# Second state-space layer: deltas from bf16 parts and a softplus read from PSUM in the scan inputs, one product block by a diagonal matrix in the scans

## Chip, core and metric

The kernel runs on one core of a Trainium2 chip. The metric is the time of one execution on the device in microseconds. The core has TensorE (PE; PEld is its weight load), VectorE (DVE), ScalarE (ACT), GpSimd (POOL) and SyncE (SP), which here only issues DMAs. Each engine takes its instructions in the order in which they are written, and the engines meet at semaphores.

## What is computed

The network has four layers on 32 images of 96 channels and 32x32 pixels. The change touches two stages of the second layer, a scan over 1024 pixels in four directions with 16 states for each of 768 channels:

```python
flat = xc.reshape(b, d, L)
flipped = xc[:, :, ::-1, ::-1].reshape(b, d, L)
xl = jnp.swapaxes(jnp.concatenate([flat, flat, flipped, flipped], axis=1), 1, 2)
A = -jnp.exp(A_log)
x_dbl = xl @ W_x                       # 6 + 16 + 16 columns
dt_r, Bm, Cm = x_dbl[..., :dr], x_dbl[..., dr:dr + n], x_dbl[..., dr + n:]
delta = jax.nn.softplus(dt_r @ W_delta + b_delta)
# for each pixel t:
dA = jnp.exp(dt[:, :, None] * A)
h = dA * h + (dt * u_t)[:, :, None] * B_t[:, None, :]
y = jnp.einsum('bdn,bn->bd', h, C_t) + Dv * u_t
```

## The kernel before

The program is a chain of stages with barriers between them; each stage loops over the 32 images.

**Scan inputs (`l1_scan_inputs`, tiles named l1p_).** The 768 channels are T = 6 tiles of 128; tiles 3 to 5 are the flipped ones and read u backwards. For an image the stage makes x_dbl on TensorE (`project`, L1258, into PSUM buffer px, in two halves of 512 pixels), copies it to SBUF on ScalarE (`read`, L1312, into dts), and makes for each tile the deltas before the softplus (`deltas`, L1265, two PSUM buffers pd). The softplus is max(x, 0) + ln(1 + exp(-|x|)): VectorE writes max(x, 0) to dl (L1228) and -|x| to ab (L1231), ScalarE does exp and ln (L1326, L1328), POOL adds the two (L1208), and VectorE multiplies by u (L1237, du). TensorE transposes du in 8 blocks (`turn_du`, L1274, into pt), ScalarE copies it out (L1320, dut), and SyncE stores dl, dut, the C rows and B. B is turned by TensorE (`turn_b`, L1280) and copied by ScalarE (L1334). The pixels of dts carry the ranks, B and C in fp32, and a product of fp32 operands is issued as two instructions for each half.

`turn(k, s)` on each engine runs through t = 0 to 5 for image k, and the function `back(k, t, lag)` says which tile stands at slot t: on TensorE the transpose of tile t-4 comes first, then the deltas of tile t+2, in slot 1 the projection of the next image, in slot 3 the turning of its B. A delta product waits until `absd` of the tile two before it, that is until VectorE has read that PSUM buffer for the last time. ScalarE's slot is: copy of tile t-5, exp and ln of t, and in slot 2 the reading of the next image's px.

**Scans (`l1_scans`, tiles named l1s_).** An image has 32 rounds (16 states, unflipped half and flipped half) of 3 tiles. For a round ScalarE makes three decays da (L1549) and eight products dm = dut x B (L1559, one for each block of 128 pixels, since B lies on the partitions there). TensorE transposes the products back, eight for each tile (L1463, into pd), VectorE scans (L1528, into h, a ring of four), POOL adds two of the three results (L1439) and multiplies twice by C (L1444, L1448), and TensorE adds these to y by products with the identity (L1473). In TensorE's order the transposes of step s+1 stand before the addition of pb (j = 1) or pa (j = 2) of the round before. After a half is done VectorE adds D times u (L1516) twice. The loop over the images is a loop of the hardware, whose body is one image.

Of the kernel before, what the change touches and what calls it, by code (L numbers as in the profile page):

```python
# [20 lines left out]
F8 = mybir.dt.float8e5  # L21
ALU = mybir.AluOpType
# [7 lines left out]
DI = 192  # L30
# [1083 lines left out]
def l1_scan_inputs(nc, u1, w, dls, duts, bts, crows, ident):  # L1114
# [4 lines left out]
    DU, TURN, OUT = 3, 4, 5  # L1119

    with ExitStack() as stack:
        r = Room(nc, "l1p", stack)
        u = r.sb("u", [128, UNROLL, 2, HW])
        dts = r.sb("dts", [128, 2, HW])
# [5 lines left out]
        wx = r.sb("wx", [128, T, 128]); wsum = r.sb("wsum", [128, 4, 128]); wd = r.sb("wd", [128, T, 128])  # L1130
# [8 lines left out]
        const, wsummed, xd, dtc, btm, btc, dtm, plus, absd, expd, lnd, sumd, dud, dutm, dutc, passed = r.step_sems(  # L1139
            "const", "wsummed", "xd", "dtc", "btm", "btc", "dtm", "plus", "absd", "expd", "lnd", "sumd", "dud", "dutm",  # L1140
            "dutc", "passed")
        consts = [(wx[:, :, :], w["wx"]), (wd[:, :, :], w["wd"]), (idt[:, :], ident)]
# [7 lines left out]
        def in_order(s, t):  # L1150
            row = u[:, s % UNROLL, U_OF[t % HT], :]
            return row[:, ::-1] if t >= HT else row

        with nc.Block() as block:
            @block.sync
            def _(sp):
# [6 lines left out]
                def turn(k, s):  # L1163
                    for t in range(T):
                        m, v = back(k, t, 3)
                        if there(m):
                            sp.wait_ge(sumd, nth(T * m + v))
                            sp.sem_inc(passed, 1)
                            sp.dma_start(one(dls[:, v], m), dl[:, v, :]).then_inc(s_dl[v], 16)
                        m, v = back(k, t, 6)  # L1170
                        if v % HT == HT - 1 and there(m):
                            g = v // HT
                            sp.wait_ge(dutc, nth(T * m + v))
# [28 lines left out]
            @block.gpsimd  # L1202
            def _(pool):
                def turn(k, s):
                    if there(k):
                        for t in range(T):
                            pool.wait_ge(lnd, nth(T * k + t))
                            pool.tensor_tensor(dl[:, t, :], dl[:, t, :], ln[:, t % 3, :], ALU.add).then_inc(sumd, 1)  # L1208

                turns(pool, turn, 1, 1)  # L1210

            @block.vector
            def _(dve):
                for rows in (slice(2 * N, 64), slice(64, 128)):
                    dve.memset(dts[rows, :, :], 1.0).then_inc(const, 1)
                dve.wait_ge(s_w, ready)
                for g in range(2):
                    dve.tensor_tensor(wsum[:, 2 * g, :], wx[:, HT * g, :], wx[:, HT * g + 1, :], ALU.add).then_inc(wsummed, 1)
                    dve.tensor_copy(wsum[:, 2 * g + 1, :], wx[:, HT * g + 2, :]).then_inc(wsummed, 1)

                def turn(k, s):
                    for t in range(T):
                        if there(k):
                            q = T * k + t
                            dve.wait_ge(s_dl[t], k * 16)
                            dve.wait_ge(dud, nth(q - T))
                            dve.wait_ge(dtm, nth(q))
                            dve.tensor_scalar(dl[:, t, :], pd[:, t % 2, :], 0.0, None, ALU.max).then_inc(plus, 1)  # L1228
                            dve.wait_ge(plus, nth(q))
                            dve.wait_ge(expd, nth(q - 3))  # L1230
                            dve.scalar_tensor_tensor(out=ab[:, t % 3, :], in0=dl[:, t, :], scalar=-2.0,  # L1231
                                                     in1=pd[:, t % 2, :], op0=ALU.mult, op1=ALU.add).then_inc(absd, 1)
                        m, v = back(k, t, DU)
                        if there(m):
                            dve.wait_ge(sumd, nth(T * m + v))
                            dve.wait_ge(dutm, nth(T * m + v - 2))
                            dve.tensor_tensor(du[:, v % 2, :], dl[:, v, :], in_order(s + (t - DU) // T, v), ALU.mult)\  # L1237
                               .then_inc(dud, 1)
# [4 lines left out]
            def _(pe):  # L1243
                pe.wait_ge(s_w, ready)
                pe.wait_ge(const, nth(1))
                pe.wait_ge(wsummed, nth(3))

                def turn(k, s):
                    p = (s + 1) % 2

                    def project():
                        pe.wait_ge(s_in[(s + 1) % UNROLL], (k + 1 - (s + 1) % UNROLL) * (16 // UNROLL) + 16)
                        pe.wait_ge(btc, nth(k))
                        for hs in HALVES:
                            for c in range(4):
                                row = u[:, (s + 1) % UNROLL, c % 2, :]
                                row = row[:, ::-1] if c >= 2 else row
                                mm = pe.matmul(px[:, hs], wsum[:, c, :], row[:, hs], start=(c == 0), stop=(c == 3))  # L1258
                        mm.then_inc(xd, 1)

                    def deltas(m, v):
                        pe.wait_ge(dtc, nth(m))
                        pe.wait_ge(absd, nth(T * m + v - 2))
                        for hs in HALVES:
                            mm = pe.matmul(pd[:, v % 2, hs], wd[:, v, :], dts[:, (s + (t + 2) // T) % 2, hs],  # L1265
# [3 lines left out]
                    def turn_du(m, v):  # L1269
                        q = T * m + v  # L1270
                        pe.wait_ge(dud, nth(q))
                        pe.wait_ge(dutc, nth(q - 1))
# [4 lines left out]
                    def turn_b():  # L1277
                        pe.wait_ge(dtc, nth(k + 1))
                        for b in range(BLOCKS):
                            mm = pe.matmul(px[:, b * N:(b + 1) * N], dts[:, p, b * 128:(b + 1) * 128], idt[:, 0:N],  # L1280
# [25 lines left out]

# [1343 lines left out]
```

## Time and profile before

| what | us |
|---|---|
| three runs | 21068.52, 21084.69 (median), 21090.51 |
| the profiled execution | 21082.77 |
| its span in the trace | 21081.0 |
| scan inputs, 9706 to 10570 | 864.0, 27.0 an image |
| scans, 10616 to 17990 | 7374.0, 230.4 an image |
| DVE, ACT, POOL, PE busy over the span | 17145.7, 16400.6, 13569.9, 18307.1 |

The two stages that the change touches are 39% of the span. The page's list of groups has the scan stage on top: 3072 scans on VectorE (6862.9 us busy), 8192 products (4459.9 us) and 3072 decays (3514.2 us) on ScalarE. Busy times of pipelined instructions overlap at their ends, so sums of durations come out above the time. Where rows carry a release ("<-PE"), it is the one that came last by the semaphores; at a loop's jump back this can name a release that had long been there.

### The profile page before, as it was taken

How to read it: one execution, taken by the hardware profiler on the slowest of the kernel's cores; microseconds unless marked ns; L12 is line 12 of the kernel's file. 1: busy time of each engine (PE TensorE's matmuls, PEld its weight loads, DVE VectorE, ACT ScalarE, POOL GpSimd, SP SyncE). 2: the span in 40 equal slices, each digit the busy share in tenths (PEclk: the TensorE clock that was granted, in tenths of full speed). 3: DMA queues.
4: the chain of work that ended last, by engine and by line, in shares of the span. 5: the costliest groups of instructions: out<-in, count | busy, mean ns of one | idle time of the engine just before them, and what ended most of it. 6: DMA issues, size and time to landing. Idle time of an engine off the chain costs nothing. (4 is left out here: it accounts for less than half of the span.)

```text
span 21081.0 us, 264592 instructions
## 1 busy us (share of the span) xinstructions
PE 18307.1 (87%) x73736; PEld 10023.1 (48%) x73736; DVE 17145.7 (81%) x12555; ACT 16400.6 (78%) x25994; POOL 13569.9 (64%) x6372
## 2 busy tenths in 40 slices
PE   7789997799985999889988998998989899789798
PEld 2345553455542344334555555555555555345353
DVE  2888888788875679748989999999999999756666
ACT  6499996799972555566799999999999999334545
POOL 0278884488861678626589999999999999100101
PEclk8799998899998999999999999999999999889899
DMA  3577775677766332276733333333333333820302
GB/s 120 189 229 219 228 229 185 208 229 220 223 206 191 106 124 78 101 251 228 272 138 123 115 124 114 125 118 121 123 115 124 114 124 117 190 68 27 89 28 83
DMA packets 842523, 3171.86 MB, mean 150 GB/s; under 512 B 101542, under 2 KB 124682, under 8 KB 816140
## 3 DMA queue, kind: packets, MB, share of 16 engines
q1 hardware_dynamic: 805900, 3030.56, 44.4%
q10 hardware_dynamic: 35328, 125.85, 1.8%
q8 instruction: 591, 9.68, 0.2%
q14 instruction: 704, 5.77, 0.1%
HBM read 2317.15 MB, written 838.88 MB: 150 GB/s over the span
## 5 line engine op out<-in xcount | busy, mean ns | idle before, releaser
L1528 DVE TENSOR_TENSOR_SCAN l1s_h<-l1s_da,l1s_pd 128x1024 f32<-128x1024 f32 x3072 | 6862.9, 2275 | 388.7 <-PE l1s_pd L1463 348.0
L1559 ACT ACTIVATE l1s_dm<-l1s_dut,l1s_bt 128x384 f32<-128x384 f32 x8192 | 4459.9, 609 | 15.9 <-DMA l1s_u<-u 11.5
L1463 PE MATMUL l1s_pd<-l1s_id,l1s_dm 128*128 128x128 f32 x24576 | 3196.2, 277 | 606.5 <-ACT l1s_dm L1559 358.6
L1463 PEld LDWEIGHTS l1s_pd<-l1s_id,l1s_dm 128*128 128x128 f32 x24576 | 2756.3, 142 | 2028.8 <-DVE l1s_h L1528 1122.7
L1549 ACT ACTIVATE l1s_da<-l1s_dl,l1s_a 128x1024 f32<-128x1024 f32 x3072 | 3514.2, 1144 | 19.1 <-DVE l1s_h L1528 18.6
L1439 POOL TENSOR_TENSOR l1s_sm<-l1s_h 128x1024 f32<-128x1024 f32 x1024 | 2429.0, 2372 | 263.8 <-DVE l1s_h L1528 253.5
L1444 POOL TENSOR_TENSOR l1s_pb<-l1s_h,l1s_cc 128x1024 f32<-128x1024 f32 x1024 | 2433.6, 2377 | 1.1
L1448 POOL TENSOR_TENSOR l1s_pa<-l1s_sm,l1s_cc 128x1024 f32<-128x1024 f32 x1024 | 2429.3, 2372 | 0.0
L852 POOL TENSOR_TENSOR dw_acc<-dw_acc,dw_prod 128x961 f32<-128x961 f32 (+3 forms) x704 | 1572.9, 2276 | 1008.2 <-ACT dw_prod L805 1000.6
L1473 PE MATMUL l1s_py<-l1s_pb,l1s_id 128*128 128x512 f32 x4096 | 1995.8, 610 | 166.3 <-POOL l1s_pb L1444 162.3
L2328 POOL TENSOR_TENSOR l0sb_pr<-l0sb_h,l0sb_cc 128x1024 f32<-128x1024 f32 x768 | 1815.8, 2365 | 434.1 <-DVE l0sb_h L2404 373.0
L2328 POOL TENSOR_TENSOR l0sf_pr<-l0sf_h,l0sf_cc 128x1024 f32<-128x1024 f32 x768 | 1815.8, 2365 | 433.7 <-DVE l0sf_h L2404 373.6
L2089 POOL CAST ffn_h<-ffn_z 128x1024 fp8e5<-128x1024 f16 x128 | 180.9, 1414 | 2897.7 <-DVE ffn_z L2109 2892.7
L1473 PE MATMUL l1s_py<-l1s_pa,l1s_id 128*128 128x512 f32 x4096 | 1927.5, 593 | 0.0
L783 PE MATMUL dw_pc<-dw_vol,dw_diag 128*128 128x512 f32 (+7 forms) x4224 | 1765.1, 581 | 57.4 <-DMA dw_vol<-n 30.4
L882 DVE SCALAR_TENSOR_TENSOR dw_pc<-dw_vol,dw_wt,dw_pc 128x961 f32<-128x961 f32 (+5 forms) x1280 | 1484.6, 1234 | 210.1 <-PE dw_pc L783 206.2
L2360 PE MATMUL l0sf_py<-l0sf_pr,l0sf_id 128*128 128x512 f32 x3072 | 1580.4, 597 | 0.0
L2360 PE MATMUL l0sb_py<-l0sb_pr,l0sb_id 128*128 128x512 f32 x3072 | 1580.3, 597 | 0.0
L2452 ACT ACTIVATE l0sf_dm<-l0sf_dut,l0sf_bt 128x192 f32<-128x192 f32 x4096 | 1500.0, 455 | 9.5 <-DMA l0sf_dl<-l0dlsf 9.5
L2452 ACT ACTIVATE l0sb_dm<-l0sb_dut,l0sb_bt 128x192 f32<-128x192 f32 x4096 | 1493.9, 447 | 9.6 <-DMA l0sb_dl<-l0dlsb 9.6
L2341 PEld LDWEIGHTS l0sb_pd<-l0sb_id,l0sb_dm 128*128 128x128 f32 x6144 | 751.7, 142 | 1105.2 <-issue 757.4
L2341 PEld LDWEIGHTS l0sf_pd<-l0sf_id,l0sf_dm 128*128 128x128 f32 x6144 | 751.5, 142 | 1105.0 <-issue 758.1
(297 smaller groups left out, 30544.0 us busy)
## 6 DMA issues: line engine op xcount, KB each, us to landing
l1s_cc<-crows SPq DMA_DIRECT2D x1024, 512.0 KB, 3.7
l0sf_cc<-l0crowsf SPq DMA_DIRECT2D x512, 512.0 KB, 5.1
l0sb_cc<-l0crowsb SPq DMA_DIRECT2D x512, 512.0 KB, 5.1
l0sf_cc<-l0crowsf SPq DMA_DIRECT2D x512, 256.0 KB, 6.6
l0sb_cc<-l0crowsb SPq DMA_DIRECT2D x512, 256.0 KB, 6.5
dls<-l1p_dl SPq DMA_DIRECT2D x192, 512.0 KB, 6.9
duts<-l1p_dut SPq DMA_DIRECT2D x64, 1536.0 KB, 5.8
l1s_dut<-duts SPq DMA_DIRECT2D x64, 1536.0 KB, 7.2
```

The lines of the kernel that those rows point to most:

```text
L783: mm = pe.matmul(pixels(pc[:, f % 4, :])[:, ys, xs], diag[:, v % tiles, diag_taps.index(tap), :], source(v, f, tap, ys, xs), start=(n == 0 ...
L1439: pool.tensor_tensor(sm[:, rnd % 2, :], h[:, rnd * HT % 4, :], h[:, (rnd * HT + 1) % 4, :], ALU.add)\
L1444: pool.tensor_tensor(pb[:, rnd % 2, :], h[:, (rnd * HT + 2) % 4, :], cc[:, rnd % 4, :], ALU.mult)\
L1448: pool.tensor_tensor(pa[:, rnd % 2, :], sm[:, rnd % 2, :], cc[:, rnd % 4, :], ALU.mult)\
L1463: mm = pe.transpose(pd[:, s % 2, blk * 128:blk * 128 + 128], dm[:, rnd % 2, blk, j * 128:j * 128 + 128], idt[:, :])
L1473: mm = pe.matmul(target[:, hs], idt[:, :], prods[:, rnd % 2, hs], start=(n == 0), stop=(n == N - 1))
L1528: dve.tensor_tensor_scan(h[:, s % 4, :], da[:, j, :], pd[:, s % 2, :], 0.0, ALU.mult, ALU.add)\
L1549: act.activation(da[:, j, :], dl[:, half, j, :], ACT.Exp, scale=a[:, HT * half + j, n:n + 1])\
L1559: ins = act.activation(dm[:, rnd % 2, blk, :], dut[:, half, blk, :], ACT.Identity, scale=bt[:, half, blk, n:n + 1])
L2328: pool.tensor_tensor(pr[:, s % 4, :], h[:, s % 6, :], cc[:, rnd % 4, j, :], ALU.mult).then_inc(prod, 1)
L2360: mm = pe.matmul(py[:, j, HALVES[half]], idt[:, :], pr[:, s % 4, HALVES[half]], start=(n == 0), stop=(n == N - 1))
L2452: ins = act.activation(dm[:, rnd % 2, blk, cols], dut[:, rnd // N, blk, cols], ACT.Identity, scale=bt[:, rnd // N, q, blk, rnd % N:rnd % N ...
```

## The change

In the scan inputs:
- The rows of dt's weights stand three times in three groups of 32 rows of the projection, with three rows of ones for the bias (`one_at`, L1306, one bf16 product more in each half). ScalarE copies all of px to bf16 (`parts`, L1358) and B and C separately (`bc`, L1361). VectorE subtracts (L1281), ScalarE rounds the rest to bf16 (L1371), VectorE subtracts again (L1284): parts then holds a high, middle and low part of each value. The deltas are one bf16 product for each half with weights `wdel` of stacked parts (L1313), made once at the stage's start on VectorE.
- VectorE sets the sign bit of the delta to get -|x| (L1263), and after exp and ln one pass reads the delta from PSUM again: max(x, 0) + ln, in two halves (L1271), into dl. A delta product now waits for these halves of the tile two before it (`sumd`).
- The product with u is POOL's (L1226). The transposes are copied out by VectorE for even tiles (L1277) and by ScalarE for odd ones (L1376), both four slots back.
- ScalarE reads px in slot 2 before exp and ln of tile 2, not behind them.

In the scans, for even states: ScalarE leaves out the product of the last block, and TensorE multiplies dut of that block by a diagonal matrix of B (L1516), made by ScalarE once for each even state of an image, in the first half (L1619). TensorE waits for blocks 0 to 3 and 4 to 7 separately (`multlo`, `multhi`).

```diff
@@ scan inputs, VectorE
-                            dve.wait_ge(dtm, nth(q))
-                            dve.tensor_scalar(dl[:, t, :], pd[:, t % 2, :], 0.0, None, ALU.max).then_inc(plus, 1)
-                            dve.wait_ge(plus, nth(q))
-                            dve.wait_ge(expd, nth(q - 3))
-                            dve.scalar_tensor_tensor(out=ab[:, t % 3, :], in0=dl[:, t, :], scalar=-2.0,
-                                                     in1=pd[:, t % 2, :], op0=ALU.mult, op1=ALU.add).then_inc(absd, 1)
-                        m, v = back(k, t, DU)
-                        if there(m):
-                            dve.wait_ge(sumd, nth(T * m + v))
-                            dve.wait_ge(dutm, nth(T * m + v - 2))
-                            dve.tensor_tensor(du[:, v % 2, :], dl[:, v, :], in_order(s + (t - DU) // T, v), ALU.mult)\
-                               .then_inc(dud, 1)
+                            dve.wait_ge(dtm, nth(q))
+                            dve.wait_ge(expd, nth(q - 3))
+                            dve.tensor_scalar(ab[:, t % 3, :].bitcast(I32), pd[:, t % 2, :].bitcast(I32), SIGN, None, ALU.bitwise_or).then_inc(absd, 1)
+                        m, v = back(k, t, 1)
+                        if there(m):
+                            q = T * m + v
+                            dve.wait_ge(lnd, nth(q))
+                            for hs in HALVES:
+                                dve.scalar_tensor_tensor(out=dl[:, v, hs], in0=pd[:, v % 2, hs], scalar=0.0,
+                                                         in1=ln[:, v % 3, hs], op0=ALU.max, op1=ALU.add).then_inc(sumd, 1)
+                        m, v = back(k, t, OUT)
+                        if v % 2 == 0 and there(m):
+                            dve.wait_ge(dutm, nth(T * m + v))
+                            dve.tensor_copy(*place(s, v)).then_inc(evened, 1)
+                        if t == 2 and there(k + 1):
+                            dve.wait_ge(hi, nth(k + 1))
+                            dve.tensor_tensor(rest[GROUPS, :], px[GROUPS, :], parts[GROUPS, p, :], ALU.subtract).then_inc(res, 1)
+                        if t == 3 and there(k + 1):
+                            dve.wait_ge(mid, nth(k + 1))
+                            dve.tensor_tensor(parts[96:128, p, :], rest[96:128, :], parts[96:128, p, :], ALU.subtract)\
+                               .then_inc(lo, 1)
@@ scan inputs, TensorE
                     def deltas(m, v):
-                        pe.wait_ge(dtc, nth(m))
-                        pe.wait_ge(absd, nth(T * m + v - 2))
-                        for hs in HALVES:
+                        pe.wait_ge(lo, nth(m))
+                        for i, hs in enumerate(HALVES):
+                            pe.wait_ge(sumd, nth(2 * (T * m + v - 2) + i))
@@ scan inputs, ScalarE: first in slot 2
+                        if t == 2 and there(k + 1):
+                            act.wait_ge(xd, nth(k + 1))
+                            act.activation(parts[:, p, :], px[:, :], ACT.Copy).then_inc(hi, 1)
+                            act.activation(bc[0:2 * N, p, :], px[0:2 * N, :], ACT.Copy).then_inc(bcd, 1)
@@ scans, TensorE and ScalarE
+                    if diagonal(n):
+                        pe.wait_ge(diagd, nth(b * (N // 2) + (N // 2 - 1 if half else n // 2)))
+                        pe.matmul(pd[:, s % 2, LAST * 128:], dut[:, half, LAST, j * 128:j * 128 + 128], bd[:, n // 2, :],
+                                  start=True, stop=True)
...
+                        if diagonal(n) and half == 0:
+                            act.activation(bd[:, n // 2, :], idt[:, :], ACT.Identity, scale=bt[:, half, LAST, n:n + 1])\
+                               .then_inc(diagd, 1)
```

TensorE in the scan-input stage, one image from the transposes of slot 1 on. Before:

```order
L1274 MATMUL l1p_pt<-l1p_id,l1p_du 128x128 x8
L1265 MATMUL l1p_pd<-l1p_dts,l1p_wd 128x512 x2
L1258 MATMUL l1p_px<-l1p_u,l1p_wsum 128x512 x8
L1274 MATMUL l1p_pt<-l1p_id,l1p_du 128x128 x8
L1265 MATMUL l1p_pd<-l1p_dts,l1p_wd 128x512 x2
L1274 MATMUL l1p_pt<-l1p_id,l1p_du 128x128 x8
L1265 MATMUL l1p_pd<-l1p_dts,l1p_wd 128x512 x2
L1280 MATMUL l1p_px<-l1p_id,l1p_dts 128x16 x8
```

And in the changed kernel:

```order
L1322 MATMUL l1p_pt<-l1p_id,l1p_du 128x128 x8
L1313 MATMUL l1p_pd<-l1p_parts,l1p_wdel 128x512 x2
L1305 MATMUL l1p_px<-l1p_u,l1p_wsum 128x512 x4
L1306 MATMUL l1p_px<-l1p_one,l1p_oneat 128x512
L1305 MATMUL l1p_px<-l1p_u,l1p_wsum 128x512 x4
L1306 MATMUL l1p_px<-l1p_one,l1p_oneat 128x512
L1322 MATMUL l1p_pt<-l1p_id,l1p_du 128x128 x8
L1313 MATMUL l1p_pd<-l1p_parts,l1p_wdel 128x512 x2
```

The places are the same: the projection still stands behind the deltas of tile 3 and ahead of the transposes of tile 4; what the deltas wait for is another thing.

ScalarE in the scan-input stage, from exp of tile 1 (before, behind the copy of its slot) to the end of slot 2. Before:

```order
L1326 ACTIVATE l1p_ln<-l1p_ab 128x1024
L1328 ACTIVATE l1p_ln<-l1p_ln 128x1024
L1320 ACTIVATE l1p_dut<-l1p_pt 128x8x128
L1326 ACTIVATE l1p_ln<-l1p_ab 128x1024
L1328 ACTIVATE l1p_ln<-l1p_ln 128x1024
L1312 ACTIVATE l1p_dts<-l1p_px 38x1024
```

And in the changed kernel:

```order
L1366 ACTIVATE l1p_ln<-l1p_ab 128x1024
L1368 ACTIVATE l1p_ln<-l1p_ln 128x1024
L1376 ACTIVATE l1p_dut<-l1p_pt 128x8x128
L1358 ACTIVATE l1p_parts<-l1p_px 128x1024
L1361 ACTIVATE l1p_bc<-l1p_px 32x1024
L1366 ACTIVATE l1p_ln<-l1p_ab 128x1024
L1368 ACTIVATE l1p_ln<-l1p_ln 128x1024
L1371 ACTIVATE l1p_parts<-l1p_rest 64x1024
```

The reading of px has moved from behind exp and ln of tile 2 to ahead of them.

VectorE in the changed scan-input stage, slots 2 to 4:

```order
L1263 TENSOR_SCALAR l1p_ab<-l1p_pd 128x1024
L1271 SCALAR_TENSOR_TENSOR l1p_dl<-l1p_pd,l1p_ln 128x512 x2
L1277 COPY l1p_dut<-l1p_pt 128x8x128
L1281 TENSOR_TENSOR l1p_rest<-l1p_px,l1p_parts 64x1024
L1263 TENSOR_SCALAR l1p_ab<-l1p_pd 128x1024
L1271 SCALAR_TENSOR_TENSOR l1p_dl<-l1p_pd,l1p_ln 128x512 x2
L1284 TENSOR_TENSOR l1p_parts<-l1p_rest,l1p_parts 32x1024
L1263 TENSOR_SCALAR l1p_ab<-l1p_pd 128x1024
L1271 SCALAR_TENSOR_TENSOR l1p_dl<-l1p_pd,l1p_ln 128x512 x2
L1277 COPY l1p_dut<-l1p_pt 128x8x128
```

Between the last pass of a tile (L1271) and the next signs (L1263) now stand, in slots 2 and 4, a copy of transposes that TensorE makes behind other work.

## Rows read from the trace of the kernel before

**Rows 1.** The three stretches as windows: us, busy us of each engine, granted clock, DMA.
```profile
core 0: us, PE busy (x) PEld busy (x) DVE busy (x) ACT busy (x) POOL busy (x), PEclk, DMA share, GB/s
800.00:1060.00 260.00, 190.68 (x714) 96.52 (x714) 221.51 (x156) 131.62 (x121) 57.82 (x25) 0.78 0.55 186
9706.00:10570.00 864.00, 786.54 (x3263) 448.35 (x3263) 777.63 (x572) 611.15 (x632) 453.45 (x191) 1.00 0.71 269
10616.00:17990.00 7374.00, 6630.38 (x32753) 4106.71 (x32751) 7000.23 (x3198) 7343.33 (x11254) 7149.51 (x3071) 1.00 0.34 119
```

**Rows 2.** Groups by line in 9680 to 10575: busy us, mean ns | idle before.
```profile
L1208 POOL TENSOR_TENSOR l1p_dl<-l1p_dl,l1p_ln 128x1024 f32<-128x1024 f32 x192 | 456.8, 2379 | 451.3 <-ACT l1p_ln L1328 451.3
L1265 PE MATMUL l1p_pd<-l1p_dts,l1p_wd 128*128 128x512 f32 x768 | 367.7, 602 | 10.4 <-DVE l1p_ab L1231 10.4
L1237 DVE TENSOR_TENSOR l1p_du<-l1p_dl,l1p_u 128x1024 f32<-128x1024 f32 x190 | 338.8, 1784 | 52.2 <-PE l1p_pt L1274 52.2
L1231 DVE SCALAR_TENSOR_TENSOR l1p_ab<-l1p_dl,l1p_pd 128x1024 f32<-128x1024 f32 x192 | 234.4, 1221 | 13.0
...
L1326 ACT ACTIVATE l1p_ln<-l1p_ab 128x1024 f32<-128x1024 f32 x192 | 202.8, 1056 | 135.1 <-DVE l1p_ab L1231 127.1 <-POOL l1p_dl L1208 7.6
```

**Rows 3.** Timeline of that stage at a projection: start us, us, engine, work [idle before].
```profile
10099.76 3.60 PE L1258 MATMUL l1p_px<-l1p_u,l1p_wsum 128*128 128x512 f32 x8
...
10103.20 1.04 PE L1274 MATMUL l1p_pt<-l1p_id,l1p_du 128*128 128x128 f32 x8
...
10104.34 1.23 DVE L1237 TENSOR_TENSOR l1p_du<-l1p_dl,l1p_u 128x1024 f32<-128x1024 f32 x1 [1.72 <-PE l1p_pt L1274]
...
10108.38 1.85 PE L1280 MATMUL l1p_px<-l1p_id,l1p_dts 128*128 128x16 f32 x16
```

**Rows 4.** A one-pass product elsewhere, by tile: duration ns min/median/max.
```profile
L2153 PE MATMUL ffn_ph<-ffn_x,ffn_w x384: 375/379/635, 19566.2 to 21068.0; 96*128 96x512 fp8e5 x192
```

**Rows 5.** Groups by line, VectorE: 512 elements in one instruction.
```profile
L1999 DVE TENSOR_TENSOR att_xo<-att_ev,att_yv 96x512 f32<-96x512 f32 x128 | 82.5, 684 | 6.6
```

**Rows 6.** Groups by line, TensorE in 560 to 1080, first layer.
```profile
L453 PE MATMUL l0pf_pd<-l0pf_dts,l0pf_wd 128*128 128x512 f32 x128 | 84.0, 793 | 0.0
...
L467 PE MATMUL l0pf_px<-l0pf_u,l0pf_wx 128*38 128x512 f32 x122 | 64.5, 610 | 0.9 <-ACT l0pf_u L525 0.9
```

**Rows 7.** Timeline of TensorE at the end of the scan-input stage, gaps and short bursts.
```profile
10574.15 1.94 PE L1274 MATMUL l1p_pt<-l1p_id,l1p_du 128*128 128x128 f32 x8 [2.63 <-ACT l1p_dut L1320]
```

**Rows 8.** Timeline of the scan stage, two rounds inside a half.
```profile
12503.33 2.36 POOL L1439 TENSOR_TENSOR l1s_sm<-l1s_h 128x1024 f32<-128x1024 f32 x1
...
12506.56 1.13 ACT L1549 ACTIVATE l1s_da<-l1s_dl,l1s_a 128x1024 f32<-128x1024 f32 x1
12506.74 6.64 DVE L1528 TENSOR_TENSOR_SCAN l1s_h<-l1s_da,l1s_pd 128x1024 f32<-128x1024 f32 x3 [0.34 <-PE l1s_pd L1463]
...
12508.07 1.98 PE L1473 MATMUL l1s_py<-l1s_pb,l1s_id 128*128 128x512 f32 x4 [0.52 <-POOL l1s_pb L1444]
...
12510.29 2.36 POOL L1439 TENSOR_TENSOR l1s_sm<-l1s_h 128x1024 f32<-128x1024 f32 x1
...
12512.21 1.61 ACT L1559 ACTIVATE l1s_dm<-l1s_dut,l1s_bt 128x384 f32<-128x384 f32 x3
...
12513.73 1.13 ACT L1549 ACTIVATE l1s_da<-l1s_dl,l1s_a 128x1024 f32<-128x1024 f32 x1
```

**Rows 9.** Timeline of the scan stage where an image begins.
```profile
12462.79 2.66 PE L1463 MATMUL l1s_pd<-l1s_id,l1s_dm 128*128 128x128 f32 x16 [2.13 <-DVE l1s_h L1528]
...
12466.53 2.37 POOL L1439 TENSOR_TENSOR l1s_sm<-l1s_h 128x1024 f32<-128x1024 f32 x1 [2.60 <-DVE l1s_h L1528]
...
12475.43 2.37 POOL L1439 TENSOR_TENSOR l1s_sm<-l1s_h 128x1024 f32<-128x1024 f32 x1 [1.88 <-DVE l1s_h L1528]
```

**Rows 10.** Timeline of the scan stage where the second half begins.
```profile
12588.54 2.36 POOL L1439 TENSOR_TENSOR l1s_sm<-l1s_h 128x1024 f32<-128x1024 f32 x1 [1.52 <-DVE l1s_h L1528]
```

**Rows 11.** Timeline of VectorE alone after that beginning of an image.
```profile
12472.99 26.44 DVE L1528 TENSOR_TENSOR_SCAN l1s_h<-l1s_da,l1s_pd 128x1024 f32<-128x1024 f32 x12
```

More of the change, by code:

```diff
@@ L1123, in l1_scan_inputs @@
         u = r.sb("u", [128, UNROLL, 2, HW])
-        dts = r.sb("dts", [128, 2, HW])
+        parts = r.sb("parts", [128, 2, HW], BF16); rest = r.sb("rest", [128, HW]); bc = r.sb("bc", [128, 2, HW])
         ab, ln = (r.sb(n, [128, 3, HW]) for n in ("ab", "ln"))
@@ L1329, in turn @@
                         if t == 2 and there(k + 1):
-                            read()
+                            act.wait_ge(res, nth(k + 1))
+                            act.activation(parts[GROUPS, p, :], rest[GROUPS, :], ACT.Copy).then_inc(mid, 1)
+                        m, v = back(k, t, OUT)
+                        if v % 2 and there(m):
+                            act.wait_ge(dutm, nth(T * m + v))
+                            act.wait_ge(s_du[v // HT], m * 16)
+                            act.activation(*place(s, v), ACT.Copy).then_inc(odded, 1)
                         if t == 4 and there(k + 1):
@@ L1342, in l1_scans @@
     BLOCKS = HW // 128
+    LAST = BLOCKS - 1
+    HALF_OF = (range(0, BLOCKS // 2), range(BLOCKS // 2, BLOCKS))
     ROUNDS = 2 * N
@@ L2515, in build @@
     dls1 = dram("dls1", (IMAGES, 6, 128, HW)); ys1 = dram("ys1", (IMAGES, 4, 128, HW))
-    ws = {n: w[f"{n}_1"] for n in ("wx", "wd", "alog", "skip", "ln_g", "ln_b", "wo")} | {"avg192": w["avg192"]}
+    ws = {n: w[f"{n}_1"] for n in ("wx", "wd", "which", "alog", "skip", "ln_g", "ln_b", "wo")} | {"avg192": w["avg192"]}
     l1_scan_inputs(nc, u1, ws, dls1, duts, bts, crows, w["ident"])
@@ L2606, in arranged @@
     w["l1dw_b"] = twice(v["L1_conv_b_dw"])
-    w["wx_1"] = tiles(cat([bc_first(v["L1_conv_W_x"])[order], np.zeros((len(order), 128 - XD), f)], 1), 6)
-    w["wd_1"] = rows_at_dt(cat([v["L1_conv_W_delta"], v["L1_conv_b_delta"][None]])[:, order].reshape(RANK + 1, 6, 128))
+    wx, wd = v["L1_conv_W_x"], np.zeros((128, 4 * DI), f)
+    thrice = [np.tile(wx[:, :RANK], 3), np.zeros((4 * DI, 32 - 3 * RANK), f)]
+    w["wx_1"] = tiles(cat([wx[:, RANK:], *thrice * 3], 1)[order], 6)
+    which = np.zeros((128, 3), f)
+    for j in range(3):
+        for group in range(3):
+            rows = slice(32 + 32 * group + RANK * j, 32 + 32 * group + RANK * (j + 1))
+            wd[rows], which[rows, j] = v["L1_conv_W_delta"], 1
+        wd[32 + 3 * RANK + j], which[32 + 3 * RANK + j, j] = v["L1_conv_b_delta"], 1
+    w["wd_1"], w["which_1"] = wd[:, order].reshape(128, 6, 128), which
     w["alog_1"] = tiles(v["L1_conv_A_log"][order], 6)
```

137 lines of the change are left out of this document (87 added, 50 removed).

## The prediction

> **What bounds the kernel now.** I read the table of windows first, to see which stretches the change touches and how full each engine is there. The second layer's scan inputs take 864.0 us for 32 images, 27.0 us each, with TensorE (786.5 us) and VectorE (777.6 us) both near 90% busy; the scans take 7374 us, 230.4 us an image, with ScalarE busy for 7343 us of it and GpSimd (POOL) for 7150 us [rows 1]. Then the groups by line, for durations and for who ends whose idle time, and last the timelines, since in both stages the order on an engine decides more than its sum.
>
> In the scan-input stage, eight projection instructions take 3.60 us, so they follow each other at 0.43 us, and all 16 of an image occupy TensorE for 6.9 us; meanwhile VectorE works on and waits only 1.72 us [rows 3]. VectorE's multiply by u takes 1784 ns on average, its other passes 1221 ns [rows 2].
>
> In the scan stage three clocks run side by side. ScalarE repeats its round of 3 decays and 8 products every 7.17 us (12506.56 to 12513.73) without a gap. POOL repeats its three operations every 6.96 us (12503.33 to 12510.29), also without a gap. VectorE's three scans take 6.64 us, and it waits 0.34 us for transposes that stand in TensorE's queue behind an addition that itself waited 0.52 us for POOL [rows 8]. So ScalarE sets the long run, but POOL is right behind it: 32 rounds of 6.97 are 223.0 us, and POOL idles 2.60 and 1.88 us where an image begins and 1.52 us at the second half [rows 9, 10], 6.0 us; only 230.4 - 223.0 - 6.0 = 1.4 us of an image is left that ScalarE alone imposes.
>
> **The change in the scans.** In 16 of 32 rounds ScalarE makes 7 products instead of 8. Three take 12513.73 - 12512.21 = 1.52 us, 0.507 each [rows 8], so 8.1 us an image go. Eight times an image it makes a 128x128 diagonal: between a decay (1.04 us from start to start for 1024 elements) and a product (0.507 for 384) an element costs 0.83 ns, so 128 elements cost about 0.29 us, 2.4 us in all. ScalarE comes to 32 x 7.17 - 8.1 + 2.4 = 223.7 us an image, below what POOL needs with its waits. POOL gets the bound, so the saving is not 5.7 us but what POOL stops losing. Where POOL leads, the first of the three scans from 12506.74 ends 2.2 us later, at 12508.9 [rows 8, 11]; POOL's sum needs it and starts at 12510.29, so POOL has 1.3 us in hand. TensorE's longer turn takes 0.2 us of that: a turn of an even state trades one transpose for two passes of a full product, and 16 such short instructions take 1.85 us, 0.11 each [rows 3], so +0.11 us for each of two turns on that path. With 1.1 us in hand, the idle of 2.60 becomes 1.5, that of 1.52 some 0.8 (part of its slack was there before), 1.88 stays, and the 1.4 us go: 3.2 us an image, rounded down to 3.1, or **-100 us** for 32. Bounds: -40 us if POOL's idle stays and only the 1.4 us go, -150 us if the slack covers both halves' idle twice. The split wait on products costs nothing, as ScalarE's products then come early.
>
> **The change in the scan inputs.** By sums it looks good: six delta products fall from 24 to 12 instructions of one pass (a one-pass 512-column product takes 379 ns, alone, against 602 [rows 2, 4]), and the multiply by u goes to POOL, which idles half the stage. VectorE has 6 sign passes at 1.13 us from start to start, 12 half passes at 0.60 (684 ns long [rows 5]), 3 copies and 2 subtractions, about 20.5 us. But the order makes a ring. Deltas of tile t+2 overwrite the buffer of tile t, now free only after the **last** pass of t, which needs ScalarE's exp and ln of t. On TensorE, deltas of tile 3 stand ahead of the projection, and they wait for the last pass of tile 1. Behind the projection stands the transpose turn of tile 4 of the image before; VectorE's next instruction after that last pass copies its result. ScalarE's next instruction after tile 1 reads the projection's result, now ahead of exp and ln of tile 2 and no longer behind them. So all three wait for the 7 us.
>
> I follow one image, from the moment at which the last pass of tile 1 ends. A hand-over between engines costs 0.05 us; an instruction that waits for nothing starts 0.09 us before the one ahead ends (12 scans of 2.28 take 26.44 [rows 11]). Full VectorE passes are 1.22, ScalarE's 1.06, copies 1.0 to 1.2.
> - TensorE: deltas 3, 16 projections at 0.43 and two one-pass products at 0.22, end 7.7; turn of tile 4, 1.04 [rows 3], 8.6.
> - ScalarE: reads the parts 8.8, B and C 9.7, exp 10.7, ln of tile 2 at 11.8.
> - VectorE: idle until 8.7; copy 9.9, first subtraction 11.0, sign of 3 at 12.1, last pass of 2 at 13.3, second subtraction 15.0, sign of 4 at 16.1, last pass of 3 at 17.3.
> - TensorE: deltas 5 at 17.8, B turned (1.85) 19.5, turn of tile 0 at 20.4. VectorE has waited since 17.3; copy 21.7, sign of 5 at 22.8, last pass of 4 at 24.0.
> - Deltas 24.4; sign 25.7, last pass of 5 at 26.9; deltas 27.3, turn of tile 2 at 28.2; copy 29.4, sign 30.5, last pass 31.7; deltas 32.2, sign 33.4, last pass of tile 1 at **34.6**.
>
> Of the 34.6 us VectorE idles 14: 8.7 under the projection, 3.1 behind B's turning, 1.4 and twice 0.5 behind turns and deltas. The multiply by u on POOL is three tiles ahead of its transposes and hidden (a POOL operation is 2379 ns [rows 2], a tile now takes over 5 us). The second subtraction has both inputs in SBUF and runs beside POOL's multiply: the old multiply with such inputs took 1784 ns on average beside POOL's additions [rows 2], so I gave it 1.8 us, between 1.2 and, behind a whole POOL operation, 3.6.
> The Trainium skill (SBUF, State Buffer, "Who interferes with whom") says that a VectorE instruction with two SBUF inputs blocks until a GpSimd operation that reads SBUF is done; by it this term is 3.6 instead of 1.8 us, and the sum 58 us higher.
>
> Last, TensorE's clock. It was 1.00 in this stage at 91% busy, but in the first layer's like stage, with gaps, 0.78 [rows 1]; its delta products took 793 ns there against 602, a third more, its projections 610 [rows 2, 6]. Here TensorE gets four gaps of 2 to 4 us an image. A third more on the short bursts on the path (six deltas of 0.4, two turns of 1.04, B's 1.85, 6.3 us in all) is 2.1 us, plus 0.3 for the projection: 2.4. So **37.0 us an image, +10.0, +320 us** for 32. Bounds: 33.5 (full clock, subtraction at 1.2, B's turning partly hidden) and 41, +208 and +448. The preparation of the weights' parts adds nine dependent VectorE instructions of 768 elements, near 1 us each by rows 5, of which the first image's load hides half: +4.
>
> **Sum.** On the profiled execution's 21082.8 us (1.9 below the median of the three runs): -100 + 320 + 4 = +224, **21307 us**.
>
> **Rivals.**
> (a) Faster: the ring is open. If TensorE gets to the projection before the other two need it, VectorE's 20.5 us with small waits sets the image. For it speaks that only 1.72 us of the projection showed on VectorE before [rows 3]; against it, that those buffers came free without ScalarE then. At 22 us the stage saves 160 us: 21083 - 160 - 100 + 4 = 20827. The point from which it decides: an image of the scan inputs under 27.0 + 3.0 = 30.0 us makes the whole faster, and one near 30 gives no change.
> (b) The clock stays at its lower level. At the end of this stage eight transposes took 1.94 us instead of 1.04, with gaps of 1 to 3 us [rows 3, 7]: 1.2 GHz, not 2.4. If all bursts run so, deltas add 1.2, B's turning 1.7, two turns 1.8, and half of the projection 3.4: 42.7 us an image, +502, hence 21489. Against it: a long projection comes every image.
> The Trainium skill (TensorE: Matmul & The Clock Gate, "Loop structure matters more than you think") says that waits between bursts drop the clock to half; by that rule this rival is the outcome.
> (c) The scans gain nothing, because POOL's waits stay and the longer turns eat the rest: 21407.
>
> **How the numbers follow.** The forecast 0.72, (a) 0.10 with the cases near no change, (b) 0.10, (c) 0.08. The range runs from 21083 + 208 - 150 = 21141, taken as 21130, up to 21450, between the stage's upper bound with the forecast's scans (21435) and (b). Within 0.2%, some 42 us, is about what a measurement of this kernel can't tell from no change: faster 0.09, same 0.03, slower 0.88.
>
> **What would show it.** Right: in the new profile the scan inputs take near 37 us an image; VectorE's copy out of the transposes shows a wait of 7 to 9 us once an image for TensorE, ScalarE's read of the parts a like one; POOL's idle grows; the granted clock there is 0.7 to 0.9. In the scans ScalarE shows idle before its decays, POOL's period stays 6.97 and its idle at an image's beginning falls. Wrong: VectorE above 80% busy in the first stage, or ScalarE still without a gap in the second. A slow copy on POOL with u read backwards, or a sign pass that is not as long as another pass from PSUM, would shift the hand count.

## The result and the profile after

The changed kernel takes 21383.9 us, median of four runs (21373.2 to 21390.4), against 21080.6 of the kernel before on the same chip (21068.5 to 21090.5): a ratio of 1.0144, 95% interval 1.0126 to 1.0161. That is 303 us slower. The forecast was 21307 us, slower by 224, in a range of 21130 to 21450.

The two stages as windows (us, busy us of each engine, granted clock, DMA share, GB/s), which answer to the last two lines of [rows 1]:

```profile
9715.00:10953.00 1238.00, 838.45 (x2942) 524.17 (x2942) 654.68 (x732) 591.82 (x603) 447.04 (x190) 0.70 0.48 188
10995.00:18286.00 7291.00, 6777.43 (x34283) 4393.86 (x34283) 6959.26 (x3198) 7171.83 (x10999) 7141.11 (x3070) 1.00 0.34 120
```

The scan inputs grew from 864 to 1238 us, with no engine above 68% busy and the clock at 0.70 where it had been 1.00. The scans shrank from 7374 to 7291.

To compare kernels I use periods, from the first to the last start of one kind of pass. The sign passes of the 192 tiles are:

```profile
L1263 DVE TENSOR_SCALAR l1p_ab<-l1p_pd x192: 1214/1225/1226, 9716.0 to 10949.3; 128x1024 int32<-128x1024 int32 x192
```

That is 1233.3 us for 191 steps, so 38.74 us an image; the same for L1231 of the kernel before gives 26.95. The scans' first to last start is 7288.9 us, before 7369.4. So the inputs cost 11.79 x 32 = +377 us, the scans give -80, and some 6 of the 303 are a remainder that lies in neither.

The waits of the scan-input stage (engine, line waited for, us in total, times, longest):

```profile
POOL l1p_du L1226 <- PE l1p_pt L1322: 737.3, 163, 23.0
DVE l1p_dut L1277 <- PE l1p_pt L1322: 512.3, 94, 10.0
...
PE l1p_pd L1313 <- DVE l1p_dl L1271: 392.0, 191, 5.0
ACT l1p_parts L1358 <- PE l1p_px L1306: 255.2, 31, 12.9
ACT l1p_ln L1366 <- DVE l1p_ab L1263: 193.5, 66, 4.0
```

VectorE waits for TensorE's transposes (16 us an image), TensorE for VectorE's last pass (12 us an image): a ring, as drawn. POOL's wait costs nothing: the whole list has no wait of another engine for `du`, which POOL writes. One image on VectorE, from copy to copy behind the projection (start, us, work, [idle before]); this answers to the hand count:

```profile
10204.42 1.23 DVE L1277 COPY l1p_dut<-l1p_pt 128x1024 f32<-128x1024 f32 x1 [9.57 <-PE l1p_pt L1322]
10205.68 1.23 DVE L1281 TENSOR_TENSOR l1p_rest<-l1p_px,l1p_parts 64x1024 f32<-64x1024 f32 x1
...
10209.51 1.22 DVE L1284 TENSOR_TENSOR l1p_parts<-l1p_rest,l1p_parts 32x1024 bf16<-32x1024 f32 x1
...
10219.03 1.23 DVE L1277 COPY l1p_dut<-l1p_pt 128x1024 f32<-128x1024 f32 x1 [5.72 <-PE l1p_pt L1322]
...
10223.38 1.22 DVE L1263 TENSOR_SCALAR l1p_ab<-l1p_pd 128x1024 int32<-128x1024 int32 x1 [0.79 <-PE l1p_pd L1313]
...
10227.95 1.22 DVE L1277 COPY l1p_dut<-l1p_pt 128x1024 f32<-128x1024 f32 x1 [2.16 <-PE l1p_pt L1322]
...
10232.30 1.22 DVE L1263 TENSOR_SCALAR l1p_ab<-l1p_pd 128x1024 int32<-128x1024 int32 x1 [0.79 <-PE l1p_pd L1313]
...
10243.37 1.23 DVE L1277 COPY l1p_dut<-l1p_pt 128x1024 f32<-128x1024 f32 x1 [8.66 <-PE l1p_pt L1322]
```

TensorE in the same image:

```profile
10203.35 1.04 PE L1322 MATMUL l1p_pt<-l1p_id,l1p_du 128*128 128x128 f32 x8
10208.94 1.21 PE L1313 MATMUL l1p_pd<-l1p_parts,l1p_wdel 128*128 128x512 bf16 x2 [4.56 <-DVE l1p_dl L1271]
...
10213.77 3.44 PE L1329 MATMUL l1p_px<-l1p_id,l1p_bc 128*128 128x16 f32 x16
10217.05 1.95 PE L1322 MATMUL l1p_pt<-l1p_id,l1p_du 128*128 128x128 f32 x8
...
10230.96 1.20 PE L1313 MATMUL l1p_pd<-l1p_parts,l1p_wdel 128*128 128x512 bf16 x2 [3.05 <-DVE l1p_dl L1271]
...
10234.17 0.99 PE L1313 MATMUL l1p_pd<-l1p_parts,l1p_wdel 128*128 128x512 bf16 x2 [0.30 <-DVE l1p_dl L1271]
10235.00 3.60 PE L1305 MATMUL l1p_px<-l1p_u,l1p_wsum 128*128 128x512 f32 x8
```

The projection runs at 2.4 GHz (eight in 3.60 us, as before), and so does the turn right behind it (1.04). After the gap of 4.56 us, and until shortly before the next projection, the short bursts run at 1.2 GHz: B's turning takes 3.44 us where it took 1.85, a turn 1.95 where it took 1.04 [rows 3].

### The profile page after: what moved, and what is told of

The parts are those of the page before. It is cut to its first block and busy times, and to the rows that moved or that the text cites. A ratio compares the mean times of both kernels' runs of the same rounds, so it can differ in the third digit from the quotient of the medians.

```text
span 21388.6 us, 270104 instructions
## 1 busy us (share of the span) xinstructions
PE 18507.4 (87%) x74952; PEld 10380.1 (49%) x74952; DVE 16989.2 (79%) x12725; ACT 16208.1 (76%) x25706; POOL 13563.5 (63%) x6372
## 5 line engine op out<-in xcount | busy, mean ns | idle before, releaser
L1625 ACT ACTIVATE l1s_dm<-l1s_dut,l1s_bt 128x384 f32<-128x384 f32 x7680 | 4189.6, 605 | 65.8 <-PE l1s_pd L1522 65.7
L1522 PE MATMUL l1s_pd<-l1s_id,l1s_dm 128*128 128x128 f32 x23040 | 3071.4, 275 | 158.5 <-DVE l1s_h L1587 84.9
L1522 PEld LDWEIGHTS l1s_pd<-l1s_id,l1s_dm 128*128 128x128 f32 x23040 | 2640.0, 142 | 829.6 <-issue 569.7
L883 DVE SCALAR_TENSOR_TENSOR dw_pc<-dw_vol,dw_wt,dw_pc 128x961 f32<-128x961 f32 (+5 forms) x1280 | 1484.9, 1238 | 209.9 <-PE dw_pc L784 205.9
```

What stands on the lines that cost most here:

```text
L1522: mm = pe.transpose(pd[:, s % 2, blk * 128:blk * 128 + 128], dm[:, rnd % 2, blk, j * 128:j * 128 + 128], idt[:, :])
L1625: ins = act.activation(dm[:, rnd % 2, blk, :], dut[:, half, blk, :], ACT.Identity, scale=bt[:, half, blk, n:n + 1])
```

## The experiments

All ratios are to the kernel before, run on the same chip.

**The two halves of the change.** One kernel has the changed scan inputs (and their weights) and the old `l1_scans`, the other the old inputs and the changed `l1_scans`.

> The changed scan inputs with the scans of before. If the two stages simply add, this has the whole loss and not the scans' gain: the scan inputs near 38.7 us an image as in the changed kernel (27.0 before), the scans at 230.4, so 21081 + 32 x 11.7 = about 21455 us. Rival: the scans' gain depends on the new inputs or the loss is partly in the scans; then this lies nearer the changed kernel's 21384.

Measured: 21457.0 us, 1.0178 (1.0161 to 1.0195), 38.75 us an image.

> The scan inputs of before with the changed scans (diagonal blocks for even states). Theory: POOL takes over the bound, an image of the scans falls from 230.4 to 227.8 us, 21081 - 83 = about 20998 us. Rival: no gain in the scans by themselves, 21081.

Measured: 20973.8 us, 0.9949 (0.9932 to 0.9965), against 21081.0: 107 us faster, 24 more than expected. The inputs alone cost 376 us. The scans give 107 us alone and 73 on top of the changed inputs; the scans alone are the fastest kernel of this study.

**Is the projection on the path?** One of four products of each half is made; three quarters of the projection are left out, so x_dbl is not whole.

```diff
-                            for c in range(4):
+                            for c in range(1):
```

> The changed kernel with the projection cut to one of its four fp32 products in each half; three of the four terms of x_dbl are left out. That takes 12 instructions of 0.43 us, 5.2 us, out of TensorE's queue at the one place. Theory: all of it is on the path, the scan inputs fall from 38.7 to about 33.5 us an image, 21384 - 165 = 21219 us, or more if the clock gains. Rival: the wait under the projection is only another wait's cover; then 50 us or less go.

Measured: 21211.4 us in a single run, 33.88 us an image. 4.9 of the 5.2 us taken away show, so nearly all of the projection lies on the path.

**Whose wait is it?** First ScalarE's place: its read of px goes back behind exp and ln of tile 2 (the diff is shortened, the brackets stand for the instructions).

```diff
-                        if t == 2 and there(k + 1):
-                            (read of parts, then of bc)
                         if there(k):
                             (exp and ln of tile t)
+                        if t == 2 and there(k + 1):
+                            (read of parts, then of bc)
```

> The changed kernel with ScalarE's reading of the projection (two copies) put back behind exp and ln of tile 2, nothing else. By the hand count VectorE's last pass of tile 2 waits for its own engine's order (12.0) as long as for ln (11.8), since it must copy and subtract first: no change, within 0.3 us an image, 21384 +- 10 us. Rival: ScalarE's place of waiting is a cause of its own (its read waits 8 us an image); then exp and ln of tile 2 leave the path, -2.1 us an image, 21317 us.

Measured: 21367.5 us, 1.0139 (1.0122 to 1.0156), 38.60 us an image. That is 16 us under the changed kernel, where 10 were allowed, but only 0.14 us an image of it lies in this stage, where the rival has 2.1. ScalarE's 8.6 us wait is real and costs next to nothing: VectorE waits for the same projection through the transposes. Then the transposes, every tile's one slot earlier, so that those of tile 4 stand ahead of the projection and those of tile 0 ahead of B's turning:

```diff
-    TURN, OUT = 4, 4
+    TURN, OUT = 3, 4
```

> The changed kernel with TensorE's transposes of a tile one slot earlier (three slots back instead of four), ahead of the deltas, the projection and the turning of B that they stood behind; no work added or taken away. Theory of the ring: VectorE's copies of even tiles no longer wait behind that work; of its waits of 9.6, 5.7 and 2.2 us an image the second and third go, the first shrinks by the copy's 1.1 us, small waits for deltas (0.8 us) appear instead: about 32 us an image of the scan inputs instead of 38.9, 21384 - 210 = 21174 us. Rival: the projection alone makes the loss; then only 1.1 us an image goes, 21350 us.

Measured: 21210.9 us, 1.0062 (1.0045 to 1.0079), 33.85 us an image. Right in kind, 37 us short in size. VectorE's long wait moved to its first subtraction, which wants ScalarE's parts; those waits come to 198.8 us in the first 25 images, 8 us each, about what was expected. A second one was not expected, for deltas that stand behind B's turning and a turn at 1.2 GHz, where 0.8 us had been put down:

```profile
10300.41 1.23 DVE L1281 TENSOR_TENSOR l1p_rest<-l1p_px,l1p_parts 64x1024 f32<-64x1024 f32 x1 [7.56 <-ACT l1p_parts L1358]
...
10316.40 1.23 DVE L1263 TENSOR_SCALAR l1p_ab<-l1p_pd 128x1024 int32<-128x1024 int32 x1 [3.26 <-PE l1p_pd L1313]
```

Then, on top of it, the projection in four pieces in four slots (the diff shows where the pieces now stand, without the edit of the projection itself and without the first image's start):

```diff
-                        if t == 1 and there(k + 1):
-                            project()
+                        if t >= 4 and there(k + 2):
+                            project(k + 2, s + 2, t - 4)
+                        if t < 2 and there(k + 1):
+                            project(k + 1, s + 1, t + 2)
```

> As the run with the early transposes, and the projection in four pieces of about 1.9 us behind the deltas of slots 4, 5, 0 and 1 instead of in one piece in slot 1. Theory of the ring: the wait of about 8 us under the projection goes, TensorE has no long gaps and keeps its clock: about 26 us an image, 21384 - 32 x 12.7 = 20980 us, faster than before. Rival: each piece stands ahead of the next transposes and deltas, so the 7 us come back as four waits: 30 us an image, about 21110 us.

Measured: 21074.9 us, 0.9997 (0.9988 to 1.0007), 29.28 us an image. Of the 11.8 us an image that the changed inputs cost, 2.3 are left without one pass taken from VectorE. But this is 95 us more than expected, and the 29.28 us are nearer to the rival's 30 than to the theory's 26. The trace does not show the rival's four waits, though. VectorE's two longest waits of an image are for deltas behind B's turning and for ScalarE's read:

```profile
10208.21 1.23 DVE L1263 TENSOR_SCALAR l1p_ab<-l1p_pd 128x1024 int32<-128x1024 int32 x1 [3.26 <-PE l1p_pd L1316]
...
10220.96 1.23 DVE L1281 TENSOR_TENSOR l1p_rest<-l1p_px,l1p_parts 64x1024 f32<-64x1024 f32 x1 [2.19 <-ACT l1p_parts L1366]
```

Last, ScalarE's read behind exp and ln of tile 2 (the diff above) and the subtractions and the rounding one slot later:

```diff
-                        if t == 2 and there(k + 1):
+                        if t == 3 and there(k + 1):
                             dve.wait_ge(hi, nth(k + 1))
...
-                        if t == 3 and there(k + 1):
+                        if t == 4 and there(k + 1):
                             dve.wait_ge(mid, nth(k + 1))
```

> As the run with the projection in pieces, and ScalarE reads the projection behind exp and ln of tile 2; VectorE's two subtractions and ScalarE's rounding stand one slot later. In that run VectorE waited 2.2 us for the read and 0.5 us for ln behind it, and TensorE idled 4 us there, after which it worked at 1.2 GHz (B's turning 3.4 us, a transpose turn 1.9). Theory: these waits go and the clock stays higher, 29.3 to about 26.3 us an image, 21075 - 95 = 20980 us. Rival: the deltas' wait for the last pass comes in their place, 21060 us.

Measured: 21027.0 us, 0.9975 (0.9965 to 0.9986), 27.86 us an image; expected were 47 us less. The read's place alone was worth 0.14 us an image in the changed kernel; the later read together with the later subtractions is worth 1.4 once the projection is off the path. How the 1.4 divide between them was not measured. What is left shows in the timeline:

```profile
10201.38 1.94 PE L1325 MATMUL l1p_pt<-l1p_id,l1p_du 128*128 128x128 f32 x8 [4.59 <-ACT l1p_dut L1384]
...
10203.40 2.35 POOL L1226 TENSOR_TENSOR l1p_du<-l1p_dl,l1p_u 128x1024 f32<-128x1024 f32 x1 [4.97 <-PE l1p_pt L1325]
10203.96 3.43 PE L1332 MATMUL l1p_px<-l1p_id,l1p_bc 128*128 128x16 f32 x16
10204.61 2.22 DVE L1284 TENSOR_TENSOR l1p_parts<-l1p_rest,l1p_parts 32x1024 bf16<-32x1024 f32 x1
```

TensorE still idles 4.59 us and then runs at 1.2 GHz, and the second subtraction takes 2.22 us beside POOL's multiply.

**What the clock costs.** Eight needless bf16 products into px, whose content is dead there, stand ahead of the deltas of slots 4 and 0, where TensorE would idle.

```diff
+                    def filler(m):
+                        pe.wait_ge(btc, nth(m))
+                        for _ in range(8):
+                            pe.matmul(px[:, 0:HALF], one_at[:, :], one_row[:, 0:HALF], start=True, stop=True)
+                        if t == 4 and there(k + 1):
+                            filler(k + 1)
+                        if t == 0 and there(k) and there(k + 1):
+                            filler(k)
```

> The changed kernel with eight needless bf16 products into the free buffer px ahead of the deltas of slots 4 and 0, in gaps of 3.05 us in which TensorE waits: 1.7 us of work at 2.4 GHz, 3.4 us at 1.2. Theory: what is missing between the hand count's 34.6 us and the measured 38.7 is TensorE's clock (granted 0.70 here); the fillers keep it up for the deltas and transposes behind them, -1.5 us an image, about 21336 us. Rival: clock level isn't moved or isn't what is missing; then the fillers overrun their gaps by 0.4 us each, 21409 us.

Measured: 21313.1 us, 1.011 (1.0093 to 1.0127): 71 us less than the changed kernel, for more work; 48 were expected. Of TensorE:

```profile
10199.63 2.70 PE L1320 MATMUL l1p_px<-l1p_one,l1p_oneat 128*128 128x512 bf16 x8
10202.89 0.39 PE L1313 MATMUL l1p_pd<-l1p_parts,l1p_wdel 128*128 128x512 bf16 x1 [0.56 <-DVE l1p_dl L1271]
10203.49 0.39 PE L1313 MATMUL l1p_pd<-l1p_parts,l1p_wdel 128*128 128x512 bf16 x1 [0.21 <-DVE l1p_dl L1271]
10203.71 1.05 PE L1327 MATMUL l1p_pt<-l1p_id,l1p_du 128*128 128x128 f32 x8
```

Around the filler a delta product takes 0.39 us and a turn 1.05. The clock over 9750 to 10500 is 0.85, and the stage 37.26 us an image, 1.5 less, as expected: 47 of the 71 us. The rest is in the scans (7265.4 us against 7288.9), which this edit doesn't touch. B's turning, with no filler near, still takes 3.43 us.

**Each half of the scan-input change alone**, with the changed scans. Of both edits only the lines of TensorE that decide what a delta product reads and waits for are shown. First the softplus without the parts:

```diff
-                        pe.wait_ge(lo, nth(m))
+                        pe.wait_ge(bcd, nth(m))
                         for i, hs in enumerate(HALVES):
                             pe.wait_ge(sumd, nth(2 * (T * m + v - 2) + i))
-                            mm = pe.matmul(pd[:, v % 2, hs], wdel[:, v, :], parts[:, (s + (t + 2) // T) % 2, hs],
+                            mm = pe.matmul(pd[:, v % 2, hs], wd[:, v, :], dts[:, (s + (t + 2) // T) % 2, hs],
```

> The second half of the scan-input change alone: sign pass, last pass from PSUM in halves, multiply by u on GpSimd, copies split between VectorE and ScalarE, but deltas from fp32 products of the fp32 ranks as before, so no subtraction, no rounding and no products of ones. The scans are the changed ones. Theory (the ring through the last pass is the loss, whatever makes the deltas): the ring stays. From the 38.7 us an image of the changed kernel go two subtractions, 2.4, and 0.4 of the projection; each of six delta products becomes four instructions 0.43 us apart, 1.7 us in place of 0.4 to 0.6, +1.2 each, +7. That is 43 us an image (41 to 46), so 21384 + 4.3 x 32 = 21520 us (21455 to 21620). Rival (subtractions, part copies and short products are the loss): at most 30 us an image, 21100 us or less.

Measured: 21469.5 us, 1.0181 (1.0164 to 1.0198), 42.06 us an image. The sign pass, the last pass from PSUM and the multiply on POOL, with the split copies, lose 15 us an image by themselves, without any part product.

Then the parts without the new softplus:

```diff
                         pe.wait_ge(lo, nth(m))
-                        for i, hs in enumerate(HALVES):
-                            pe.wait_ge(sumd, nth(2 * (T * m + v - 2) + i))
+                        pe.wait_ge(absd, nth(T * m + v - 2))
+                        for hs in HALVES:
```

> The first half of the scan-input change alone: deltas from nine stacked bf16 part products, with copies, subtractions and rounding, but the softplus, the sum on GpSimd, the multiply by u on VectorE and the copies of the transposes on ScalarE as before; a delta product waits for the -|x| pass again. The scans are the changed ones. Theory (the ring is the loss, and it is not there): VectorE, about 90% busy in 27.0 us an image before, gets two subtractions of 1.22 us, the second up to 2.2 beside GpSimd, so 29.4 to 30.4 us an image less what shorter products save; I take 29.5, +2.5 x 32 = +80, with scans at -90 and +4 of preparation: 21081 - 6 = 21075 us (21040 to 21115). Rival (the parts are the loss): over 34 us an image, 21220 us or more.

Measured: 21146.7 us, 1.003 (1.0019 to 1.0042), 32.21 us an image: 32 us above the range and 73 below the rival. The estimate lacked a wait of VectorE:

```profile
10208.81 1.02 ACT L1349 ACTIVATE l1p_parts<-l1p_px 128x1024 bf16<-128x1024 f32 x1 [6.89 <-PE l1p_px L1290]
...
10209.86 1.23 DVE L1265 TENSOR_TENSOR l1p_rest<-l1p_px,l1p_parts 64x1024 f32<-64x1024 f32 x1 [5.34 <-ACT l1p_parts L1349]
```

One more kernel reads late here too, with the two diffs of the last kernel of the ring:

> The kernel of the bf16 part products alone, once more, with ScalarE's read of the parts and of B and C behind exp and ln of tile 2 and both subtractions and the rounding one slot later. In the run before it, 32.2 us an image where 29.5 were expected, ScalarE waited 6.9 us for the projection ahead of exp of tile 2 and VectorE 5.3 us for ScalarE's copy ahead of its first subtraction. Theory (that wait is what was missing in the estimate): with the read late, the projection is over when VectorE comes to the subtraction; 32.2 less some 3 to 4 us of the wait that is not made up elsewhere, 28.2 to 29.2 us an image, so 21147 - 3.5 x 32 = 21035 us (21020 to 21060). Rival (what is missing is TensorE at its lower clock and VectorE's passes beside GpSimd): the wait only moves, 31.5 us an image or more, 21125 us or more.

Measured: 21085.2 us, 1.0004 (0.9995 to 1.0014), 30.33 us an image, between the 28.2 to 29.2 expected and the rival's 31.5. The 5.3 us are gone, but only 1.9 came back, since another wait took their place (TensorE first, then VectorE):

```profile
10202.11 5.15 PE L1289 MATMUL l1p_px<-l1p_u,l1p_wsum 128*128 128x512 f32 x8
...
10212.11 1.22 DVE L1260 TENSOR_TENSOR l1p_du<-l1p_dl,l1p_u 128x1024 f32<-128x1024 f32 x1 [3.17 <-PE l1p_pt L1306]
...
10217.03 2.60 DVE L1260 TENSOR_TENSOR l1p_du<-l1p_dl,l1p_u 128x1024 f32<-128x1024 f32 x1
```

With shorter delta products and the new waits TensorE rests more, and the first eight instructions of the projection take 5.15 us against 3.60. VectorE's multiply by u, which needs the turn behind it to free du, waits 3.17 us. The two halves cost 15.1 and 5.3 us an image alone and 11.8 together: in the ring each delta product stands on the path, and there the bf16 products (579 ns on average, two a tile) are shorter than the fp32 ones (800 ns in the softplus kernel, four a tile). That this makes up the whole difference was not measured.

## Why the prediction was right, point by point

**The ring.** It holds, with all three members that the hand count named: deltas of tile 3 behind the last pass of tile 1, the projection behind them (4.9 of 5.2 us when it is cut), the turn of tile 4 behind the projection (4.9 us an image when the turns go one slot ahead, tile 0's with it). ScalarE's read is behind the projection as well, but the theory gave it more weight than it has: 0.14 us an image. Rival (a), the open ring, is out: VectorE is busy for 53% of the stage.

**The hand count: 34.6 plus 2.4 us, measured 38.74.** The waits, predicted 8.7, 3.1, 1.4, 0.5 and 0.5, are 8.66, 5.72, 2.16, 0.79 and 0.79 in the image shown. The one under the projection is right to 0.05 here; in half of the images it is 8.7 and in the others 9.6 to 9.8, as in the one before this. The others are 4.0 us longer, all behind short bursts at 1.2 GHz. So the term that was mis-sized is **the clock, 2.4 us and in truth 4.0**: I took a third more for short bursts, from the delta products of the first layer [rows 2, 6], where [rows 7] had shown a turn of this very stage at nearly twice its time, 1.94 us. Rival (b) had about this size for them (4.7) but slowed the projection too, and that stayed at 2.4 GHz.
The Trainium skill (TensorE: Matmul & The Clock Gate, "Loop structure matters more than you think") says that long waits between products drop the clock to half; the trace agrees behind the gap of 4.56 us (1.95 and 3.44 us for the bursts). The projection is no exception to it: between the gap of 3.05 us and its start TensorE worked 4.0 us with one rest of 0.30, and its eight instructions take 3.60 us.

**The passes.** They were 20.4 us in the count, and 38.95 - 18.1 = 20.8 in the image shown. The second subtraction was priced at 1.8 us and takes 1.22:

```profile
L1284 DVE TENSOR_TENSOR l1p_parts<-l1p_rest,l1p_parts 32x1024 bf16<-32x1024 f32 x32 | 39.1, 1222 | 2.1 <-ACT l1p_parts L1371 1.1
```

POOL is waiting for a turn at that moment. The error was in the neighbour more than in the price: when the edits brought POOL's multiply beside it, it took 2.22 us. The 0.6 us too much are more than offset, which is luck for the total: in the stretch behind the projection passes start 1.26 us apart (10204.42, 10205.68, 10206.94), where they are 1.14 apart later and in my count. Why was not looked into.
The Trainium skill (SBUF — State Buffer, "Who interferes with whom") has such a VectorE instruction wait for POOL; the 2.22 us in the last kernel of the ring, with a start 1.2 us after POOL's and an end 1.1 after POOL's end, agree, and the 3.6 us that I had put down to it did not occur.

**The scans: -100 us, measured -80 in the changed kernel and -107 alone.** The pieces are as drawn, which also rules out rival (c). An image's beginning in the changed kernel:

```profile
13962.49 1.63 ACT L1625 ACTIVATE l1s_dm<-l1s_dut,l1s_bt 128x384 f32<-128x384 f32 x3 [1.87 <-PE l1s_pd L1522]
13962.51 2.37 POOL L1491 TENSOR_TENSOR l1s_sm<-l1s_h 128x1024 f32<-128x1024 f32 x1 [1.06 <-DVE l1s_h L1587]
...
13965.07 2.37 POOL L1496 TENSOR_TENSOR l1s_pb<-l1s_h,l1s_cc 128x1024 f32<-128x1024 f32 x1 [0.19 <-DVE l1s_h L1587]
...
13971.61 1.15 ACT L1608 ACTIVATE l1s_da<-l1s_dl,l1s_a 128x1024 f32<-128x1024 f32 x1 [0.59 <-DVE l1s_h L1587]
...
13971.74 2.37 POOL L1491 TENSOR_TENSOR l1s_sm<-l1s_h 128x1024 f32<-128x1024 f32 x1 [1.98 <-DVE l1s_h L1587]
```

POOL's 2.60 became 1.06 + 0.19 (predicted 1.5), its 1.88 is 1.98 (stays), its 1.52 at the second half is 0.91 (0.8), and ScalarE now idles, 1.87 and 0.59 us here. The engine that sets the end is POOL, with its 6.97 us a round unchanged.

**The start.** No run shows the 4 us of the weights' preparation. It is seven instructions and not nine, from 9694.72 to 9700.29, and the first projection waits for it; yet from the stage's first VectorE instruction to its first sign pass go 27.5 us (9688.52 to 9716.0), and 27.4 to the same pass of the kernel before (9684.49 to 9711.9). The remainder of 6 us lies elsewhere. The two profiled executions are 307.6 us apart, of which the stages leave 4.1 ahead of the first sign pass, -1.1 between the stages and 9.6 behind the scans, in code that the change does not touch.

So the sum of 224 lacks 79 us: about 57 from the inputs (11.79 - 10.0 = 1.79 us an image x 32), 20 from the scans, 2 from the remainder.

**Open.** The same scan code takes between 7263.4 and 7289 us in the kernels of this study (7263.5 behind the old inputs, 7288.9 behind the changed, 7265.4 with the filler). POOL's waits over 11200 to 17800 are 135 us in the changed kernel and 114 with the old inputs, so most of the 25 us is POOL waiting where an image or a half begins; why was not found. A third buffer for the deltas, which would cut the ring at its root, was not tried.

## What to carry to other kernels

Before a pass moves to where it frees a buffer later, follow the ring by hand: who needs that buffer, what stands behind that instruction on its engine, and who waits for that. Sums of busy time said 20.5 us an image, the ring said 37, and 38.7 came out. Price short TensorE bursts that follow gaps of some microseconds at the duration of the nearest such burst in the trace, which was nearly twice the busy one here. A long run is not safe either: the first eight projection instructions took 3.60 us in the changed kernel and 5.15 with the parts alone. A placement that is worth nothing while another wait ends later (ScalarE's read, 0.14 us an image) can be worth something once that wait is gone (1.4 and 1.9 here, the subtractions moved with it).

## What the hardware showed unexpectedly

Sixteen needless products an image made the stage 1.5 us an image faster, with the granted clock of TensorE at 0.85 instead of 0.70 and a turn near them at 1.05 us instead of 1.95. And relief can cost: with bf16 delta products, in the kernels of the parts alone, the granted clock of the stage was 0.77 and 0.73 instead of 1.00, and the first eight instructions of the projection took 5.15 us instead of 3.60. These kernels also add waits of VectorE, so how much of that is due to the shorter products was not measured.
